# Wide TensorE products in halves, grouped items taken apart, and every engine's order made anew, in a delta-rule attention block with a gated feed-forward

## What is computed

```python
q, k, v = (silu(causal_conv4(xn @ W)) for W in (Wq, Wk, Wv))   # 4 heads of 128
beta = sigmoid(xn @ Wb)
q, k = l2norm(q), l2norm(k); v, kb = v * beta, k * beta
# delta rule: unit lower triangular inverse of each chunk, then the state
u, w = inv(1 + strict_lower(kb @ k.T)) @ (v, kb)
u -= w @ S;  o = q @ S + lower(q @ k.T) @ u;  S += k.T @ u
# three depthwise causal convolutions of v, of 3, 15 and 31 taps, then two mixes
ms = (concat(conv3(v), conv15(v), conv31(v)) @ kernel_mix) @ channel_mixer
# gate: an MLP over xn and mean |ms|, mean |o|, mean |v| of each head
wts = softmax(gelu(features @ w1 + b1) @ w2 + b2)              # 3 weights a head
attn = rmsnorm(wts[0] * ms + wts[1] * o + wts[2] * v) @ Wo
ffn = sigmoid(mix_r(xn) @ W_r.T) * (relu(mix_k(xn) @ W_k.T) ** 2 @ W_v.T)
```

## Time and profile before

| | |
|---|---|
| median of 3 runs | 3512.97 us |
| the three runs | 3495.07, 3512.97, 3515.34 us |
| profiled execution, span | 3507.7 us |
| mean granted TensorE clock | 0.984 |
| TensorE busy | 3329.3 us |
| VectorE busy | 3165.0 us |
| ScalarE busy | 2760.5 us |
| GpSimd busy | 826.6 us |
| one turn of the loop, from one `inverse_W` to the next, mean of 29 | 107.05 us |

### The profile page before, as it was taken

The page is one execution under the profiler, slowest core; times in us unless marked ns, Lnnn a source line. Parts: engine busy times, 40 slices in busy tenths (PEclk is TensorE's granted clock), DMA queues, the critical chain, the costliest instruction groups (busy, mean ns, idle before and its releaser), DMA issues.

```text
span 3507.7 us, 70018 instructions
## 1 busy us (share of the span) xinstructions
PE 3329.3 (95%) x22880; PEld 2457.7 (70%) x22880; DVE 3165.0 (90%) x7841; ACT 2760.5 (79%) x9146; POOL 826.6 (24%) x1501
## 2 busy tenths in 40 slices
PE   7999999999999999999999999999999999999988
PEld 6666777677776677776677766777766777766764
DVE  6998999999988999899999989999899999999994
ACT  5777888777887778887788877788877788777775
POOL 3322221122221222211222212222112222122211
PEclk9999999999999999999999999999999999999999
DMA  6012211122211222111222112222112221112211
GB/s 187 19 39 51 51 40 34 29 51 51 50 32 29 42 51 51 38 35 29 51 51 49 32 26 46 51 51 41 33 29 51 51 50 33 33 38 51 45 30 21
DMA packets 188307, 154.92 MB, mean 44 GB/s; under 512 B 111804, under 2 KB 146108, under 8 KB 187688
## 3 DMA queue, kind: packets, MB, share of 16 engines
q0 software_dynamic: 31744, 79.70, 13.2%
q1 hardware_dynamic: 156200, 70.76, 7.7%
HBM read 51.34 MB, written 52.95 MB: 30 GB/s over the span
## 4 chain that ended last, share of the span: by engine, by line
PE 35%; ACT 22%; DVE 21%; issue 9%; DMA 8%; POOL 4%; SPq 0%; ACTq 0%; DVEq 0%; POOLq 0%
DVE my L1804 16%; PE dense L798 7%; PE dense L732 5%; PE dense L736 5%; DMA my<-prod 5%; PE dense L720 3%; ACT my L1272 3%; PE small L748 2%; ACT dense L1302 2%; PE cell L702 2%; DMA rows_out<-Bm 2%; PE cell L703 2%; PE cell L695 2%; POOL Xu L464 1%; DMA Bu<-rows_out 1%
## 5 line engine op out<-in xcount | busy, mean ns | idle before, releaser
L1804 DVE SCALAR_TENSOR_TENSOR my<-vT,mw,my 128x256 f32<-128x256 f32 x5408 | 2256.4, 482 | 38.3 <-DMA my<-prod 19.9
L422 POOL TENSOR_SCALAR vare<-xsq 128x2 f32<-128x2 f32 x32 | 6.0, 188 | 2026.7 <-ACT xsh L1022 2026.7
L798 PE MATMUL dense<-xsh,w 128*128 128x256 f32 x2016 | 474.5, 381 | 3.8
L798 PEld LDWEIGHTS dense<-xsh,w 128*128 128x128 f32 x2016 | 362.6, 190 | 70.9 <-ACT xr L1334 10.9
L1245 ACT ACTIVATE ka<-dense 128x512 f32<-128x512 f32 x64 | 38.2, 597 | 309.0 <-PE dense L720 309.0
L720 PE MATMUL dense<-xk,wfk 128*128 128x256 f32 x1024 | 245.3, 394 | 16.7 <-DVE xb L1864 14.3
L720 PEld LDWEIGHTS dense<-xk,wfk 128*128 128x128 f32 x1024 | 195.9, 196 | 67.2 <-issue 40.5
L574 PE MATMUL front<-xsh,wq 128*128 128x256 f32 x1024 | 237.6, 385 | 0.6 <-ACT raw L1060 0.6
L732 PE MATMUL dense<-wr,xr 128*128 128x512 f32 x512 | 235.3, 603 | 0.0
L574 PE MATMUL front<-xsh,wv 128*128 128x256 f32 x1024 | 229.9, 382 | 2.7 <-ACT xsh L1037 2.7
L736 PE MATMUL dense<-wfv,ka 128*128 128x512 f32 x512 | 230.2, 592 | 0.0
(11 more groups left out here) (188 smaller groups left out, 6855.9 us busy)
## 6 DMA issues: line engine op xcount, KB each, us to landing
my<-prod POOLq DMA_DIRECT2D x160, 384.0 KB, 4.2
xa<-in_x SPq DMA_DIRECT2D x32, 512.0 KB, 4.4
rows_out<-Bm SPq DMA_DIRECT2D x64, 256.0 KB, 4.2
out<-xb POOLq DMA_DIRECT2D x32, 512.0 KB, 14.8
Yq<-units_out SPq DMA_DIRECT2D x128, 32.0 KB, 2.3
w<-in_w SPq DMA_DIRECT2D x1, 2048.0 KB, 16.7
Bu<-rows_out SPq DMA_DIRECT2D x32, 64.0 KB, 3.0
units_out<-Xu SPq DMA_DIRECT2D x32, 64.0 KB, 2.5
```

The lines of the kernel that those rows point to most:

```text
L798: e.matmul(by_batch(o), w1[:, k, hs(2 * pair + c)], xsh[s % 2][:, k, :, 1:1 + P], start=(k == 0), stop=False)
L1804: i = e.scalar_tensor_tensor(o, vT[s % 2][:, c, :, off:off + P], mw[:, col:col + 1], o, ALU.mult, ALU.add)
```

## The change

It does not change what is computed, nor the number of instructions on any engine. Four things are done.

1. TensorE's wide items are cut in two, and the order places the halves singly: `project(s, pair, c)`, `ffn_key(s, pair, c)` and `hidden(s, pair, c)` by 256-column block, `channel_mix(s, b, part)`, `attend(s, b, part)`, and `gate_out`/`value_out(s, b, part)` (formerly together `ffn_out(s, b)`) by two of the four k.
2. Groups on ScalarE and VectorE become single items: `sum_tokens`, `copy_bq`, `sum_o`, `sum_ms`, `mix_half(s, j)`; `short_conv(s, pair, t)`, `norms_add`/`norms_inv`, six softmax items, `mix_in(s, j, c)`.
3. Some waits become looser with that: `ffn_key` waits for the four k-mixes alone (which now come first), the first half of `channel_mix` for `kernel_mix(1)` alone, and the sums of `o` and `ms` rather than the copies wait for `f_rest`.
4. The order of every engine is another, in the loop, in the prologue and at the end.

```diff
-            def ffn_key(s, pair):
-                if s == 0:
-                    e.wait_ge(ffn_in, 48)
-                e.wait_ge(*mixed_in.upto(s))
-                if s:
-                    e.wait_ge(*xb_done.upto(s - 1, pair))
-                for c in range(2):
-                    for k in range(CB):
-                        i = e.matmul(dense[pair][:, c * W:(c + 1) * W], wfk[:, k, hs(2 * pair + c)], xk[:, k, :],
-                                     start=(k == 0), stop=(k == CB - 1))
-                i.then_inc(key_mm.sem, 1)
+            def ffn_key(s, pair, c):
+                if c == 0:
+                    if s == 0:
+                        e.wait_ge(ffn_in, 48)
+                    e.wait_ge(*mixed_in.upto(s, CB - 1))
+                    if s:
+                        e.wait_ge(*xb_done.upto(s - 1, pair))
                 for k in range(CB):
+                    i = e.matmul(dense[pair][:, c * W:(c + 1) * W], wfk[:, k, hs(2 * pair + c)], xk[:, k, :],
+                                 start=(k == 0), stop=(k == CB - 1))
+                if c == 1:
+                    i.then_inc(key_mm.sem, 1)
...
+            def gate_out(s, b, part):
+                if part == 0:
+                    e.wait_ge(*mixed_in.upto(s))
+                    if b == 0:
+                        e.wait_ge(*key_relu.upto(s, 0))
+                    else:
+                        e.wait_ge(*gated.upto(s, 0))
+                for k in range(2 * part, 2 * part + 2):
                     i = e.matmul(dense[0][:, :], xr[:, k, hs(b)], wr[:, k, :], start=(k == 0), stop=(k == CB - 1))
-                i.then_inc(gate_mm.sem, 1)
-                e.wait_ge(*key_done.upto(s))
-                for k in range(CB):
+                if part == 1:
+                    i.then_inc(gate_mm.sem, 1)
...
             for i in range(2, NS):
-                deviation(i)
                 norms_k(i - 1)
                 clear_units(i - 1)
+                deviation(i)
                 add_taps(i - 1, 2, 0)
-                norms_q(i - 1)
                 add_taps(i - 1, 3, 0)
                 invert_units(i - 1, 0, 3)
                 invert_units(i - 1, 3, 5)
+                add_taps(i - 1, 3, 1)
                 invert_units(i - 1, 5, 7)
-                add_taps(i - 1, 3, 1)
+                invert_units(i - 1, 7, 9)
                 invert_o(i - 2, 0)
                 invert_o(i - 2, 1)
-                invert_units(i - 1, 7, 9)
                 add_taps(i - 1, 3, 2)
```

More of the change, by code:

```diff
@@ new lines, in vector_program @@
+            short_conv(0, 4, 3)
+            short_conv(0, 5, 2)
+            short_conv(0, 5, 3)
+            taps(0, 1, 16, 17)
+            taps(0, 2, 2, 3)
+            taps(0, 1, 15, 16)
+            taps(0, 2, 0, 1)
+            taps(0, 1, 18, 19)
+            taps(0, 2, 3, 4)
+            taps(0, 2, 6, 7)
+            taps(0, 2, 9, 10)
+            taps(0, 1, 17, 18)
+            taps(0, 1, 20, 21)
+            taps(0, 1, 22, 23)
+            norms_add(0)
+            norms_inv(0)
+            taps(0, 1, 19, 20)
@@ new lines, in vector_program @@
+            taps(NS - 2, 3, 44, 45)
+            taps(NS - 2, 3, 30, 31)
+            taps(NS - 2, 3, 25, 26)
+            taps(NS - 2, 3, 33, 34)
+            taps(NS - 2, 3, 28, 29)
+            taps(NS - 2, 3, 36, 37)
+            subtract_state(NS - 2, 1)
+            short_conv(NS - 1, 0, 2)
+            taps(NS - 2, 3, 31, 32)
+            gate_value(NS - 2, 0)
+            subtract_state(NS - 2, 0)
+            taps(NS - 2, 3, 39, 40)
+            taps(NS - 2, 3, 42, 43)
+            taps(NS - 2, 3, 45, 46)
```

1484 lines of the change are left out of this document (823 added, 661 removed).

## The result

The changed kernel takes 3556.64 us (median of 4 runs, 3555.25 to 3558.16), against 3513.09 us before: a ratio of 1.0126, 95% interval 1.0099 to 1.0152. It is 1.3% slower. The profiled execution has a span of 3554.7 us, 47.0 more than that of before. The forecast was 3468 us.

The account below looks back on a forecast made before the run. TensorE, busy 95% of the span, was taken as the bound. Loop 33 us plus ends 11 make 44: 3507.7 becomes 3464 profiled, 5 below the median, so about 3468 us; range 3390 to 3515.

Parts of the forecast that it names:

- The first part of the turn: inverse_W to end of channel_mix: halves remove waits at inverse_Z, half_X and key_state; 43.16 us becomes 42.7.
- The second part: End of channel_mix to end of scale_B: new waits at turn_features and turn_logits, scale_B sooner; 28.63 us becomes 28.8.
- The third part: End of scale_B to next inverse_W, chain over GpSimd: GpSimd waits 0.8 us for a product; 33.64 becomes 34.4.
- The falls of the clock: Half-clock windows behind TensorE's weakly used stretches would cease; mean loop turn 107.05 us becomes 105.9, 33 us in all.
- rival (b): Falls stay, moving to logits, turn_logits and gram; turn 107.5 us, median 3515, no difference; chance 0.2.
- The ends: Last turn and tail gain 9 us, prologue 2: 11 us together, bounds 0 and 20.
- rival (c): GpSimd chain lengthens: a late product for add_taps(3, 1) delays inverse_W; a 4.93 us wait gives 3588; chance 0.1.
- VectorE's busy time: Sign of being wrong altogether: VectorE's busy time rises, since no change in its taps' duration was priced.
- Rival (d): ScalarE's table load behind scale_B costs more than its row, about 1.3 us; GpSimd waits 2.1; 3506 us; chance 0.05.
- (a): Loop waits vanish and no new ones come: turn some 102.8 us, median 3379; chance 0.2 together with a middle case.

Follow-up runs that it names:

- e9: Changed kernel with eight VectorE convolution taps reordered in the loop, so four directly follow the tap whose sum they add to: 3567.28 us, ratio 1.0171.
- e11: Changed kernel with e9's edit, exp_logits moved ahead of first_taps(2) and scale_B, and turn_tokens(2) ahead of turn_logits: 3535.99 us, ratio 1.0084.
- e14: e11 with GpSimd's add_taps(3, 1) put back behind the sixth pair of the block inversion: 3499.95 us, ratio 0.9961.
- e7: Changed kernel with TensorE's turn_tokens(2) put back between logits and turn_logits in the loop: 3545.91 us, ratio 1.0086.

## Why the prediction was wrong

**The first part of the turn: right.** 42.7 was forecast, 42.76 measured; all three waits went.

**The second part: right within 0.3.** 28.8 forecast, 29.04 measured, with the waits named at `turn_logits` (0.73 of "up to 0.9") and `turn_features` (0.36).

**The third part: near by luck.** I had 34.4 and it is 34.86, for other reasons. Three things about that step were wrong.

First, it says "Here TensorE isn't the last to end". In the kernel before, TensorE was the last: `inverse_W` had 0.77 us of slack behind the blocks, so that my 0.8 would have been hidden almost whole.

Second, the sum put 0.8 us on the wait for the product of `add_taps(3, 1)`, and in the changed kernel that wait is not there. The product was ready 12.96 us behind `scale_B`, where I had 12.9, but GpSimd came to the DMA at 14.3 and not at 11.9, since L456 took 2.3 us more. Mend L456 (e9, e11) and the wait appears; put the DMA back (e14) and it goes, for 36 us.

Third, and this is the step that failed here: "GpSimd's share is the same instructions with one of them moved". I had priced VectorE's new order at nothing, and it decided how long GpSimd's instruction takes: 2.65 us for 0.35. GpSimd ended 2.2 us later, of which 0.8 were slack, and the blocks' way back over DRAM took 0.4 less in this turn. `inverse_W` itself waited little (0.2 us in the clean turn), since `turn_o` and `kernel_mix(1)` had taken most of the time that TensorE was ahead. The wait of `turn_o` was nowhere in my sum; the change had taken `project(i, 4)` from between its two parts.

**Why VectorE can hold GpSimd up.** The Trainium skill, "SBUF — State Buffer", section Who interferes with whom, says that VectorE and GpSimd share one port pair, and that whoever issues first has it for the whole instruction while the other is blocked; the section SBUF: two separate sides counts a VectorE instruction with two SBUF inputs among those that contend with a GpSimd instruction that reads SBUF. The trace agrees that L456 is held while such taps run (2.65 us for 0.35). It does not bear out that the hold ends with the one tap that was first: L456 stood from 1265.92 to 1268.57, over six whole taps, until VectorE paused.

**The falls of the clock: wrong, and the largest term.** "I take it that the clock doesn't fall there any more" holds for the inversion, where none of the 18 starts. But "The new waits (`turn_logits`, `inverse_W`) have dense work on both sides" was the failing half. `turn_logits` has small products in front of it for 3 us, 6 falls start there, and e7 shows that a cover of 0.6 us takes them away. The other 12 start at the two `turn_o`, whose waits the prediction didn't name. Two of the 17 falls before stood there too, when `turn_o` waited less. This is rival (b), at its place for a third of the falls.

The size was off as well. The 33 us of the loop's gain were wholly this term, taken as 107.05 less one of the shortest turns without a fall. In the kernel before the clock is low for 61.4 us of the loop, and at half speed that loses at most 31 us, 1.06 a turn and not 1.62; so even with no fall left, at most 31 us were to be had, less 14 for the half microsecond a turn by which I had the clean turn longer.

**The ends: wrong in sign.** I had 11 us of gain, they cost 13 in the trace. The first `inverse_W` comes at 97.0 us, 87.5 before. It is rival (c) in the prologue: GpSimd waits for the product of `add_taps(0, 3, 1)` in the middle of the block inversion. Its row after, and before:

```profile
73.88 0.91 POOL L482 DMA_DIRECT2D my<-prod  x1 [5.53 <-ACT prod L1372]
```

```profile
68.09 0.92 POOL L482 DMA_DIRECT2D my<-prod  x1 [3.17 <-ACT prod L1283]
```

The blocks are done 7.5 us later for a start 3.5 later, a wait 2.4 longer and slower steps. I had not followed this chain in the prologue at all.

**VectorE's busy time.** "I would be wrong altogether if VectorE's busy time rose": it rose by 47 us, by the 476 more taps that follow on their neighbour's sum. That sign pointed the right way, at the duration of the taps. Where it hurt was the one stretch in which they got denser.

**Rival (d): out.** In the rows above the load starts 0.01 us behind the end of `normalize`, when ScalarE was busy, and the exp 0.02 us behind the load. The same holds for 97 of the 98 loads in each of the two traces: none shows more than 0.1 us on either side.

**The balance.** Forecast against measured, in the profiled execution: the three parts of the clean turn +0.76 us x 29 = 22, what lies above that clean turn 1.56 x 29 = 45 (falls, and the longer ones among the other turns), ends 24, together 91, which is 3554.7 - 3464. The case that came true is (b), with the small lengthening that I had forecast for the clean turn made larger by L456, and (c) in the prologue only.

Two slips in the sums of the rivals change nothing of this: an eighth of the 3.37 us that are idle makes (a) 102.5 us and not 102.8, and three quarters of 0.45 are 0.34 and not 0.36.
